# Group 0 of the first pair as eight plain block products, and its kept weights made at the pair's end

## What is computed

```python
# stage 1, per batch, weights picked by language id
h      = relu(x @ W1[lang] + b1[lang])                 # 512 -> 128
u      = x + h @ W2[lang] + b2[lang]                   # 128 -> 512
x1     = x + layernorm(u) * gamma[lang] + beta[lang]
# stage 2: one W1 for all batches; the last 128 output columns by expert id
g      = gelu(x1 @ W1 + b1)                            # 512 -> 2048
out    = x1 + concat(g @ W2 + b2, g @ We[expert] + be[expert])
```

## Time and profile before

| | |
|---|---|
| three runs | 1462.78, 1464.78, 1465.11 us, median 1464.78 |
| the profiled execution | 1462.67 us, its span 1460.7 us |
| TensorE busy | 1444.1 us, 99% of the span |
| VectorE, GpSimd, ScalarE busy | 943.1, 649.3, 521.8 us |
| granted TensorE clock | 1.00 |
| DMA | 263.29 MB, 180 GB/s in the mean |

### The profile page before, as it was taken

One profiled execution on the slowest core, in us unless ns is written; L12 is line 12 of the kernel. 1 busy time (PEld: TensorE's weight loads), 2 busy tenths in 40 slices (PEclk: granted clock), 3 DMA queues, 4 the chain that ended last, 5 costly groups with the idle time before them and its releaser, 6 DMA issues.

```text
span 1460.7 us, 19098 instructions
## 1 busy us (share of the span) xinstructions
PE 1444.1 (99%) x6444; PEld 1183.9 (81%) x6444; DVE 943.1 (65%) x1604; ACT 521.8 (36%) x847; POOL 649.3 (44%) x635
## 2 busy tenths in 40 slices
PE   8899999999999999999999999999999999999999
PEld 5677788888888888888888888888888888888887
DVE  6998774766657656677556675576755676554443
ACT  3634353322432234423253323523333322432231
POOL 5895454532454524635147351383314743242101
PEclk9999999999999999999999999999999999999999
DMA  7756477553665535655355644556446464364332
GB/s 217 251 183 226 173 242 255 171 182 124 227 223 162 193 125 181 223 170 195 131 179 210 199 165 158 186 189 205 155 156 225 159 204 158 109 216 155 133 109 87
DMA packets 126328, 263.29 MB, mean 180 GB/s; under 512 B 11540, under 2 KB 83476, under 8 KB 118040
## 3 DMA queue, kind: packets, MB, share of 16 engines
q1 hardware_dynamic: 116292, 156.16, 33.7%
q10 hardware_dynamic: 9940, 105.92, 18.7%
HBM read 224.29 MB, written 37.75 MB: 179 GB/s over the span
## 4 chain that ended last, share of the span: by engine, by line
PE 91%; DVE 4%; issue 2%; POOL 2%; ACT 1%; ACTq 1%; DMA 0%; DVEq 0%; SPq 0%; POOLq 0%
PE down L226 15%; PE down L228 15%; PE down L227 15%; PE up_b L226 5%; PE up_b L228 5%; PE up_b L227 5%; PE up_c L226 4%; PE up_c L228 4%; PE up_c L227 4%; PE up_a L227 3%; PE up_a L226 3%; PE up_a L228 3%; DVE g L737 1%; PE aux L226 1%; PE aux L227 1%
## 5 line engine op out<-in xcount | busy, mean ns | idle before, releaser
L226 PE MATMUL down<-w,g 128*128 128x512 f32 x1024 | 401.2, 392 | 0.7 <-DVE g L737 0.7
L228 PE MATMUL down<-w,g 128*128 128x512 f32 x1024 | 398.9, 390 | 0.0
L227 PE MATMUL down<-w,g 128*128 128x512 f32 x1024 | 398.7, 389 | 0.0
L1050 POOL TENSOR_TENSOR w<-w_raw,ones 128x256 fp32r<-128x256 f32 x128 | 89.7, 701 | 630.1 <-DMA w_raw<-m_we 630.1
L226 PEld LDWEIGHTS down<-w,g 128*128 128x128 f32 x1024 | 192.3, 188 | 41.6 <-DVE g L737 2.6
L228 PEld LDWEIGHTS down<-w,g 128*128 128x128 f32 x1024 | 192.2, 188 | 40.3
L227 PEld LDWEIGHTS down<-w,g 128*128 128x128 f32 x1024 | 192.4, 188 | 39.0
L737 DVE TENSOR_TENSOR g<-g_raw,g 128x512 fp32r<-128x512 f32 x256 | 206.1, 822 | 24.6 <-ACT g L559 22.2
L557 ACT ACTIVATE g_raw<-up_a,m_b_sb 128x512 f32<-128x512 f32 x64 | 44.1, 690 | 411.1 <-PE up_a L228 384.7
L732 DVE TENSOR_TENSOR g_raw<-up_b,s 128x512 f32<-128x512 f32 x64 | 44.2, 691 | 224.2 <-PE up_b L228 180.1
L559 ACT CAST g<-g_raw 128x512 fp32r<-128x512 f32 x256 | 159.1, 622 | 8.1
(11 more groups left out here) (208 smaller groups left out, 2496.4 us busy)
## 6 DMA issues: line engine op xcount, KB each, us to landing
w<-w_kept ACTq DMA_DIRECT2D x56, 1792.0 KB, 7.4
w<-w_kept SPq DMA_DIRECT2D x56, 768.0 KB, 5.0
w_raw<-m_we SPq DMA_DIRECT2D x128, 128.0 KB, 4.6
out<-resid SPq DMA_DIRECT2D x64, 256.0 KB, 5.4
xTs_raw<-xT SPq DMA_DIRECT2D x56, 256.0 KB, 3.0
w_kept<-w SPq DMA_DIRECT2D x8, 1792.0 KB, 7.3
xs<-x SPq DMA_DIRECT2D x56, 256.0 KB, 4.8
aw_raw<-a_w SPq DMA_DIRECT2D x30, 256.0 KB, 4.9
```

What stands on the lines that cost most here:

```text
L226: eng.matmul(bank, a_hi, b_hi, start=opens, stop=False, skip_group_check=True)
L227: eng.matmul(bank, a_hi, b_lo, start=False, stop=False, skip_group_check=True)
L228: return eng.matmul(bank, a_lo, b_hi, start=False, stop=closes, skip_group_check=True)
L1050: eng.tensor_tensor(hi, values, ones[:, :, :].to_broadcast([P, 2, PART]), ALU.mult).then_inc(pool_eh[b], 1)
```

## The change

Group 0 of the first pair is no longer computed with seven products but with the eight plain ones. It then needs no sums of weights or of B blocks, only the high and low parts of A11, A12, A21, A22 and B11, B21, B12, B22. The products of the first batch (C11, C21) stand among the transposes of the second. The low parts of B11 and B21 are now made in PSUM: TensorE adds minus the identity times the high part to the transposed tile, and ScalarE copies the rest out (`pe_first_low`, `act_first_low`). The four C tiles lie in banks `up_a`, `down[2]`, `down[1]`, `aux`, and gelu reads them there, in the order C11, C21, C12, C22. B12 and A21 use the places of T4 and S1. T1 to T4 are still made, for group 1; T4 from a copy of B21 in `resid`. The steps of group 1 have an order of their own on ScalarE and DVE (`act_second_step`, `dve_second_step`).

The seven-part weights of group 0, which the pairs after need, are made in step k = 7 as the eighth round of the loop (`k % GROUPS` names it), stored then, and stay in slot 0 for pair 1, which no longer loads them. The core of the diff (semaphores of the seven-product groups are counted one lower, by `seven`):

```diff
+    def seven(i, n):
+        return max(0, i.count(GROUPS, n) - 1)
...
-    FIRST_B11, FIRST_B12, FIRST_B22 = (down[1], down[2]), (down[3], up_b), (aux, down[0])
-    FIRST_B21 = (down[1], down[2])
+    FIRST_B11, FIRST_B21 = (up_a, down[1]), (down[2], down[1])
+    FIRST_B12, FIRST_B22 = (down[3], up_b), (up_c, down[0])
+    FIRST_C = up_a, down[2], down[1], aux
...
+    def first_hi(eng, tile, of_w, of_x, c, opens):
+        s = slice(c * P, (c + 1) * P)
+        x_hi = bo[:, of_x, c, HI, :]
+        eng.matmul(FIRST_C[tile][:, :], w1[:, 0, HI, of_w, s], x_hi, start=opens, stop=False, skip_group_check=True)
+        eng.matmul(FIRST_C[tile][:, :], w1[:, 0, LO, of_w, s], x_hi, start=False, stop=False, skip_group_check=True)
...
+    def first_lo(eng, tile, of_w, of_x, c, closes):
+        s = slice(c * P, (c + 1) * P)
+        last = eng.matmul(FIRST_C[tile][:, :], w1[:, 0, HI, of_w, s], bo[:, of_x, c, LO, :], start=False,
+                          stop=closes, skip_group_check=True)
+        if closes:
+            last.then_inc(pe_first, 1)
...
+    def pe_first_transpose(eng, of, c, bank):
+        for t in range(TT):
+            col = (of == B21) * 2 * P + c * P
+            last = eng.matmul(bank[:, t * P:(t + 1) * P], x1[:, 0, t, col:col + P], ident[:, :], is_transpose=True,
+                              start=t == 0, stop=False, skip_group_check=True)
+        last.then_inc(pe_tr[0], 1)
+    def pe_first_low(eng, of, c, bank):
+        n = b_count(first, of, c)
+        eng.wait_ge(act_minus, 1)
+        eng.wait_ge(act_kept, n)
+        eng.wait_ge(act_bhi, n)
+        eng.matmul(bank[:, :], minus[:, :], bo[:, of, c, HI, :], start=False, stop=True,
+                   skip_group_check=True).then_inc(pe_lo, 1)
...
     def pe_first_group(eng, i):
-        eng.wait_ge(pool_w1, 2)
...
-        pe_p4(eng, i, 0)
+        for c in range(2):
+            eng.wait_ge(act_first_b12, c + 1)
+            first_hi(eng, C12, A11, B12, c, c == 0)
+            first_hi(eng, C22, A21, B12, c, c == 0)
+        for c in range(2):
+            eng.wait_ge(dve_first_b12, c + 1)
+            first_lo(eng, C12, A11, B12, c, False)
+            first_lo(eng, C22, A21, B12, c, False)
+        for c in range(2):
+            eng.wait_ge(act_bhi, b_count(i, B22, c))
+            first_hi(eng, C12, A12, B22, c, False)
+            first_hi(eng, C22, A22, B22, c, False)
+        for c in range(2):
+            eng.wait_ge(b_low, b_count(i, B22, c))
+            first_lo(eng, C12, A12, B22, c, c == 1)
+            first_lo(eng, C22, A22, B22, c, c == 1)
...
+    def act_first_part(eng, of, c, bank):
+        eng.wait_ge(pe_tr[0], b_count(first, of, c))
+        kept = t1[:, c, :] if of == B11 else b21_raw(c)
+        eng.copy(kept, bank[:, :]).then_inc(act_kept, 1)
+        eng.copy(bo[:, of, c, HI, :], bank[:, :]).then_inc(act_bhi, 1)
+    def act_first_low(eng, of, c, bank):
+        eng.wait_ge(pe_lo, b_count(first, of, c))
+        eng.copy(bo[:, of, c, LO, :], bank[:, :]).then_inc(b_low, 1)
...
+    def act_second_step(eng, i, m):
+        act_first_sum(eng, i, 1)
+        act_g(eng, i, 0, C22)
+        act_w2_hi(eng, 0)
+        act_w2_hi(eng, 1)
+        act_g(eng, i, 1, C11)
+        act_w1_hi(eng, 2)
+        act_t_hi(eng, i, T4, 0)
+        act_t_hi(eng, i, T4, 1)
+        act_xT_hi(eng, m, 0, 2)
+        act_xT_hi(eng, m, 0, 3)
+        act_aw_hi(eng, m, 0, 1)
+        act_g(eng, i, 1, C12)
+        act_g(eng, i, 1, C22)
...
-        if m and k == GROUPS - 1:
+        if m and k == GROUPS - 1 and i is not first:
             load_w1(eng, m, 0)
...
-        if i is first and 0 < k < GROUPS - 1:
+        act_g(eng, i, k, C11)
+        if i is first:
             act_w1_hi(eng, k + 1)
...
+    def dve_first_t4(eng, c):
+        eng.wait_ge(pe_first, 4)
+        eng.wait_ge(act_kept, 2 + c + 1)
+        eng.wait_ge(dve_t, t_order(first).index((T2, c)) + 1)
+        eng.tensor_tensor(bo_raw[:, T4, c, LO, :], b21_raw(c), t2_raw(c), ALU.subtract).then_inc(dve_t, 1)
...
+    def dve_second_step(eng, i, m):
+        dve_sum_q(eng, i, 1)
+        dve_sum_u2(eng, i, 1)
+        dve_g_lo(eng, i, 0, C11)
+        dve_g_lo(eng, i, 0, C21)
+        dve_w2_lo(eng, 0)
+        dve_first_t4(eng, 0)
+        dve_first_t4(eng, 1)
+        dve_sum_c12(eng, i, 1)
+        dve_sum_c22(eng, i, 1)
+        dve_g_lo(eng, i, 0, C12)
+        dve_g_lo(eng, i, 0, C22)
+        dve_w2_lo(eng, 1)
+        dve_g_lo(eng, i, 1, C11)
+        dve_xT_lo(eng, m, 0, 2)
+        dve_xT_lo(eng, m, 0, 3)
+        dve_w1_lo(eng, 2)
...
-        if i is first and 0 < k < GROUPS - 1:
+        if i is first:
             dve_w1_lo(eng, k + 1)
...
         if k == 0:
+            for of, c in t_order(i)[:4]:
+                pool_t_lo(eng, i, of, c)
             pool_aw_lo(eng, m, 0, 0)
+            pool_t_lo(eng, i, T3, 0)
+            pool_t_lo(eng, i, T3, 1)
             pool_expert(eng, i, 0, 0)
-            pool_expert(eng, i, 1, 0)
+            return
...
-        if 1 <= k < GROUPS - 1:
-            pool_weight_sums(eng, k + 1)
+        pool_weight_sums(eng, k + 1)
         if k == 1:
+            pool_t_lo(eng, i, T4, 0)
+            pool_t_lo(eng, i, T4, 1)
+            pool_expert(eng, i, 1, 0)
             pool_aw_lo(eng, m, 0, 1)
             pool_expert(eng, i, 0, 1)
...
+        if k > 2:
+            eng.wait_ge(pe_p[4], k - 2)
+            eng.wait_ge(kept_w1[k % 2], 16 * ((k - 1) // 2))
+        w, of = w1_raw[:, k % 2, LO], k % GROUPS
...
         if i is first:
             keep_w2(eng, GROUPS - 1)
+            keep_w1(eng, GROUPS)
...
-            eng.wait_ge(dve_x1, TT)
+                if t == 1:
+                    eng.wait_ge(dve_x1, TT)
+                    for c in range(2):
+                        pe_first_transpose(eng, B11, c, FIRST_B11[c])
+                if t == 2:
+                    for c in range(2):
+                        pe_first_low(eng, B11, c, FIRST_B11[c])
+            pe_first_transpose(eng, B21, 0, FIRST_B21[0])
+            pe_first_b12(eng, 0)
+            eng.wait_ge(b_low, 2)
+            pe_first_transpose(eng, B21, 1, FIRST_B21[1])
+            eng.wait_ge(pool_w1, 2)
+            first_half(eng, C11, A11, B11, True, False)
+            pe_first_b12(eng, 1)
             for c in range(2):
-                pe_transpose(eng, first, 0, c, FIRST_B11[c])
...
-                    last = eng.transpose(FIRST_B12[c][:, t * P:(t + 1) * P], x1[:, 1, t, c * P:(c + 1) * P], ident[:, :])
-                    if t == TT - 1:
-                        last.then_inc(pe_tr[1], 1)
+                pe_first_low(eng, B21, c, FIRST_B21[c])
+            pe_first_b12(eng, 2)
+            first_half(eng, C21, A21, B11, True, False)
+            pe_first_b12(eng, 3)
             for c in range(2):
                 pe_transpose(eng, first, 1, 2 + c, FIRST_B22[c])
+            eng.wait_ge(b_low, 4)
+            first_half(eng, C11, A12, B21, False, True)
+            first_half(eng, C21, A22, B21, False, True)
...
-            act_first_x_copy(eng, 2)
+            for t in range(3):
+                act_first_x_copy(eng, t)
+            act_w1_hi(eng, 1)
             act_first_x_copy(eng, 3)
-            act_first_b11(eng, 0)
...
+            for c in range(2):
+                act_first_part(eng, B11, c, FIRST_B11[c])
+            for c in range(2):
+                act_first_low(eng, B11, c, FIRST_B11[c])
+            for c in range(2):
+                act_first_part(eng, B21, c, FIRST_B21[c])
+            for c in range(2):
+                act_first_low(eng, B21, c, FIRST_B21[c])
+            act_first_b12_hi(eng, 0)
+            act_first_b12_hi(eng, 1)
+            act_b22_hi(eng, first, 0, FIRST_B22[0])
+            act_b22_hi(eng, first, 1, FIRST_B22[1])
+            for c in range(2):
+                act_t_hi(eng, first, T1, c)
+                act_b12_copy(eng, first, c, FIRST_B12[c])
+            for c in range(2):
+                act_xT_hi(eng, pairs[1], 0, c)
+            act_aw_hi(eng, pairs[1], 0, 0)
             eng.wait_ge(in_const, 16)
-            act_t_hi(eng, first, T2, 0)
-            act_first_sum(eng, first, 0)
-            act_t_hi(eng, first, T2, 1)
...
             act_g(eng, first, 0, C11)
-            act_t_hi(eng, first, T4, 0)
-            act_t_hi(eng, first, T4, 1)
-            act_w2_hi(eng, 0)
+            for c in range(2):
+                act_t_hi(eng, first, T2, c)
+            act_g(eng, first, 0, C21)
+            for c in range(2):
+                act_t_hi(eng, first, T3, c)
+            act_g(eng, first, 0, C12)
...
-            dve_t4(eng, first, 1, FIRST_B21[1])
+            for c in range(2):
+                dve_first_b12_lo(eng, c)
+                dve_first_t1(eng, c)
+            for c in range(2):
+                dve_b_lo(eng, first, B22, c, FIRST_B22[c])
+            dve_second_w1_lo(eng)
+            for c in range(2):
+                dve_t2(eng, first, c, FIRST_B22[c])
```

(4 more changed lines are left out.)

402 lines of the change are left out of this document (196 added, 206 removed).

## The result

| kernel | median us | runs | range |
|---|---|---|---|
| before | 1464.82 | 4 | 1462.78 to 1465.11 |
| changed | 1474.38 | 4 | 1473.23 to 1475.90 |

The ratio is 1.0069, 95% interval [1.0051, 1.0086]: slower by 9.6 us where 3.4 was forecast, and outside the range given. Two later comparisons gave 1.0054 [1.0033, 1.0075] and 1.0067 [1.0053, 1.0081].

What follows compares the result with a forecast made beforehand. TensorE, busy 1444.1 of 1460.7 us, was taken to bound the kernel, with GpSimd 0.5 us behind in the first pair. +1.3 (GpSimd) and +2.1 (pair's end) made +3.4, forecast 1468.0 us, range 1463.0 to 1472.0.

Steps and rivals of the forecast that it cites:

- The first group: Group 0 on TensorE: fewer waits, 2.3 us more matmuls; group 1's P1 starts at 45.8 instead of 49.37, 3.6 early.
- GpSimd's hold: First pair: GpSimd's T4 at 60.3, second batch's adapter weights at 85.4 against 84.07; TensorE waits, net 1.3 us later.
- the old sequence: GpSimd's unchanged list after T4 and the second expert, up to the adapter weights: 21.2 us, as from 62.84 to 84.07.
- the second rival: Not slower: GpSimd has the adapter weights by 82.2, residuals take 6.85 instead of 8.18; 1462.6 us; chance 0.12.
- The upper bound: GpSimd before T4 stretched times 1.6: T4 at 63.0, adapter weights at 88.1, a loss of 4.0 us.
- T4's reading from SBUF: T4's DVE subtraction reads B21 from SBUF, not PSUM; by the skill's rule it costs GpSimd up to 1.2 us.
- The pair's end: Making group 0's weights at k = 7 adds an unhidden DVE subtraction before what TensorE awaits: 2.1 us, between 1.95 and 3.11.
- the sentence apart: At the pair's end, the skill's rule would make DVE's added subtraction cost 1.95 plus most of 1.28, about 3.0 us.
- The granted clock is 1.00 in the stretch of the earlier trace and I see no reason for it to fall.: TensorE's clock assumed to stay at 1.00, so no term for a lower clock entered the sum.
- rival 3: Much slower: the new dependence pushes the adapter weights to 88.1, +4.0, and the pair's end takes 3.0; 1471.8 us; chance 0.12.
- The two signs named for being wrong: TensorE passing the adapter product before 82 us, or pair 1's B21 transposes no later than 126.2 us after it.

Runs made afterwards that it cites:

- stall_before: Kernel before, low part of the second batch's adapter weights moved behind four weight sums, lengthening TensorE's stop; 1472.77 us, ratio 1.0050 to the kernel before.
- ring: Changed kernel, ScalarE's T4 high part, xT and adapter-weight casts moved ahead of the 1792-wide weight cast; 1470.27 us, ratio 1.0036 to the kernel before.
- aw_early: Changed kernel, GpSimd's low part of the second batch's adapter weights moved directly behind the first batch's residuals; 1472.09 us, ratio 1.0045 to the kernel before.
- end_gone: Changed kernel without making group 0's kept weights at the pair's end, so part of the computation is left out; 1468.01 us, ratio 1.0019 to the kernel before.
- fill_one: Changed kernel plus 16 unread matmuls in TensorE's stop before the second batch's adapter product; 1472.23 us, ratio 1.0044 to the kernel before.
- fill_all: Changed kernel plus 7, 16 and 8 unread matmuls in three of TensorE's stops; 1471.51 us, ratio 1.0045 to the kernel before.
- again2: The changed kernel unaltered, run once more on the same chip as the measure for three filled stops; 1474.26 us, ratio 1.0067 to the kernel before.

## Why the prediction was wrong

**The first group: right.** P1 of group 1 was forecast for 45.8 us. It starts at 47.31, 45.86 when the 1.45 of the start is taken off. On the way to it TensorE waits 0.27 and 0.51 only, both for ScalarE's high parts of B11.

**GpSimd's hold: right mechanism, 2.0 for 1.3, and the size partly by luck.** T4's low part was forecast for 60.3 and came at 62.23 - 1.45 = 60.8, right behind ScalarE's casts; the stop is 4.14 (3 to 5 forecast); TensorE goes on at 86.2 by the old start (85.4 forecast). stall_before, ring and aw_early show it to be GpSimd's. But two terms of that sum were off and cancelled. T4 and the second expert took 6.6 us (62.23 to 68.80), not 3.9, one row of the expert alone 2.40; and "the old sequence", 21.2 in the sum, took 18.8 (68.80 to 87.56), for the four residuals took 6.83, not 8.18, which the second rival had named. The upper bound has a slip: 44.4, 10.6 times 1.6 and 2.2 make 63.6, not 63.0. T4's reading from SBUF shows in DVE's row (2.37 for two at 56.12, where it was 1.28), but GpSimd's four sums beside it took 4.6 us (55.34 to 59.90), little more than the 4.2 of the earlier trace rows.

**The pair's end: the term "I take 2.1" was too small.** The waits are 1.90 and 1.14, 2.75 more than the 0.29 of the earlier trace rows; end_gone gives 3.1 in B. DVE's subtraction was stretched to 3.13 at 204.79 beside GpSimd's T1, not 2.02 as at the earlier trace rows: the nearest row was that of 66.81 in the earlier trace rows. That one instruction is the whole price: it took 3.04 to DVE's next. The two g behind it are stretched too (3.46, beside GpSimd's T3 and T2), but they took 3.48 in the kernel before. The Trainium skill's rule (SBUF — State Buffer, "Who interferes with whom") had given about 3.0 here, in the sentence apart, and the trace agrees with it.

**The step that failed: "The granted clock is 1.00 in the stretch of the earlier trace rows and I see no reason for it to fall."** I forecast a stop of four microseconds myself and priced it at its length. fill_one shows 1.6 us of slow matmuls behind it; behind the pair's end five matmuls and four transposes took 2.99 us, 1.3 more than the 1.65 in the kernel before; fill_all against again2 gives 2.7 for the clock in all. The trace of before has no stop over 1.7 us and stays at 1.00, and a stop of four microseconds lies outside of what it shows. The forecast looked at where the clock was, not at what kept it there. The Trainium skill (TensorE: Matmul & The Clock Gate, Part 1) says that the array's clock is gated to half by how little the array has done just before, in these two steps only; the trace agrees, with 0.50 behind the stop of 4.14 and 1.00 before it. The prediction should have weighed that rule and did not.

**A stop not forecast.** TensorE waits 1.8 us for DVE's xT low parts at 64.25 (0.2 before). Being ahead of GpSimd, it paid for it from its lead.

The sum: 2.0 (GpSimd) + 2.75 (end) + 2.7 (clock) = 7.5 us, of 9.2 to 10.0 that the three pairs of medians differ by (7.9 to 10.1 by their ratios). At the place of pair 1 the first profile is 8.2 behind, of which 2.0 (GpSimd), 2.75 (end) and the two slow stretches of 1.6 and 1.3 make 7.7. About 2 us of the difference of the medians are left that I can't assign. Part may lie in C, where profiles of one kernel differ by 1.4 us and more. Of 85 executions of the kernel before, 32 have a mean granted clock of 1.000 and a median of 1464.4 us, 12 have 0.997 and 1469.2; of the changed kernel's 14 none is above 0.997. The changed kernel has slow stretches always, the one before now and then. In the kernel before, 0.003 of the mean clock go with 4.8 us; the changed kernel's mean is 0.0036 lower (0.9953 against 0.9989), which at that rate would be 5.8 us. That is an estimate from above, since some of its slow time costs nothing, but it leaves room for the clock to hold the rest as well; no run shows it.

The rivals: rival 3 (much slower, 1471.8) had the pair's end at 3.0, which came, and the weights at 88.1, of which 86.2 came; without a price for the clock it too was short. The two signs named for being wrong did not come: TensorE passed the adapter product at 87.61, 86.2 by the old start, not before 82, and the transposes of B21 lie 131.0 behind it, later than 126.2. Both were made to catch a time below the forecast, and neither could catch one above it. What shows the miss is that 131.0 is more than 126.2 + 2.1, and that the matmuls in between follow at 0.43.
